# A graph network kernel in which SP, with single-row DMAs, brings one of the 68 gathered tiles of each iteration

## The reference

```
edge_index = jnp.stack([src, dst])
h = jnp.maximum(_layernorm(x, axis=-1), 0.0)
x = x + _L0_gnn_ref(h, edge_index, W_rel, W_root, b_rel)      # agg = segment_sum(h[src], dst); agg @ W_rel.T + b + h @ W_root.T
h = jnp.maximum(_layernorm(x, axis=-1), 0.0)
x = x + _L1_gnn_ref(h, edge_index, edge_attr_50, ...)         # below, with h as its x
edge_weights = jax.nn.silu(edge_features @ We1 + be1) @ We2 + be2
messages = x[src] * edge_weights
agg = jax.ops.segment_sum(messages, dst, num_segments=x.shape[0])
out = jax.nn.silu(agg @ Wn1 + bn1) @ Wn2 + bn2
return x + out
```

## Time and profile before

| | |
|---|---|
| time, median of 3 runs | 5621.94 us (5613.85 to 5627.18) |
| span of the profiled execution | 3996.3 us |
| layer 0, first to last gather issued | 3.5 to 1964.1 us |
| layer 1, first to last gather issued | 2011.3 to 3976.7 us |
| POOL busy | 2976.2 us (74%) |
| PE busy | 2447.1 us (61%) |
| DVE busy | 1995.0 us (50%) |
| ACT busy | 1187.2 us (30%) |

### The profile page before, as it was taken

How to read it: one execution, slowest core, us unless ns; L and a number is a source line. 1 busy time by engine, 2 the same in 40 slices (tenths; PEclk the granted TensorE clock), 3 DMA queues, 4 the chain that set the end, 5 groups by cost and what they waited for, 6 DMA issues and landing times.

```text
span 3996.3 us, 52113 instructions
## 1 busy us (share of the span) xinstructions
PE 2447.1 (61%) x10946; PEld 1882.0 (47%) x10946; DVE 1995.0 (50%) x6931; ACT 1187.2 (30%) x2730; POOL 2976.2 (74%) x3135
## 2 busy tenths in 40 slices
PE   3444444444444444444467788877887777887787
PEld 2334333333433333433445555555555555555555
DVE  6555555555555555555554444444444444444444
ACT  3444444444444444444411111111111111111111
POOL 7777777777777777777567777777777777777776
PEclk8555555555555555555578788788788887888878
DMA  2222222222222222222122222222222222222222
GB/s 84 62 61 61 61 64 67 61 61 61 61 64 67 61 61 61 61 66 64 50 78 78 83 80 79 81 76 83 78 80 82 77 75 83 80 79 82 77 76 82
DMA packets 208083, 284.73 MB, mean 71 GB/s; under 512 B 70338, under 2 KB 137972, under 8 KB 207828
## 3 DMA queue, kind: packets, MB, share of 16 engines
q0 software_dynamic: 100096, 205.20, 18.1%
q1 hardware_dynamic: 66676, 58.00, 4.9%
q10 hardware_dynamic: 41184, 20.45, 1.7%
HBM read 262.97 MB, written 20.45 MB: 71 GB/s over the span
## 4 chain that ended last, share of the span: by engine, by line
POOL 67%; issue 23%; PE 5%; DMA 2%; DVE 1%; POOLq 1%; ACT 0%; SPq 0%; DVEq 0%; ACTq 0%
POOL rows L298 67%; PE hid_ps L368 2%; PE seg_a L330 1%; PE ew_ps L373 1%; DMA rows<-h_rows,idx 1%; PE seg_b L330 1%; DMA ef<-ef_blocks 1%; POOLq L176 1%; POOLq L177 0%; DVE rows L670 0%; DVE onehot L566 0%; DVE ew_ps L666 0%; ACT hidden L502 0%; PE node_t L382 0%; ACT rows L436 0%
## 5 line engine op out<-in xcount | busy, mean ns | idle before, releaser
L298 POOL DMA_INDIRECT rows<-h_rows,idx x1564 | 1490.0, 953 | 522.6 <-issue 515.6
L298 POOL DMA_INDIRECT rows<-x,idx x1564 | 1485.2, 950 | 478.2 <-issue 478.2
L330 PE MATMUL seg_a<-onehot,rows 128*128 128x128 f32 x3312 | 726.6, 388 | 915.0 <-DVE onehot L566 408.1
L330 PEld LDWEIGHTS seg_a<-onehot,rows 128*128 128x128 f32 x3312 | 623.7, 281 | 1148.5 <-issue 960.0
L330 PE MATMUL seg_b<-onehot,rows 128*128 128x128 f32 x2944 | 606.4, 370 | 530.9 <-DVE onehot L566 374.4
L424 ACT ACTIVATE rows<-rows,e_shift,e_rstd 128x128 f32<-128x128 f32 x1564 | 643.3, 481 | 793.0 <-DVE e_shift L593 793.0
L330 PEld LDWEIGHTS seg_b<-onehot,rows 128*128 128x128 f32 x2944 | 520.8, 266 | 727.6 <-issue 448.3
L502 ACT ACTIVATE hidden<-hid_ps,be_col 128x512 f32<-128x512 f32 x391 | 268.8, 687 | 1416.1 <-PE hid_ps L368 1415.8
L373 PE MATMUL ew_ps<-we_sb,hidden 128*128 128x128 f32 x3128 | 539.8, 330 | 49.1 <-ACT hidden L502 49.1
L582 DVE BATCH_NORM_STATS2 e_stats<-rows 128x6 f32<-128x128 f32 x1564 | 339.7, 280 | 426.1 <-DMA rows<-x,idx 361.8
L368 PE MATMUL hid_ps<-ef,we_sb 50*128 50x512 f32 x782 | 522.7, 753 | 39.4 <-DMA ef<-ef_blocks 39.4
(11 more groups left out here) (91 smaller groups left out, 811.5 us busy)
## 6 DMA issues: line engine op xcount, KB each, us to landing
ef<-ef_blocks SPq DMA_DIRECT2D x391, 100.0 KB
rows<-x,idx POOLq DMA_INDIRECT x1564, 2.5
rows<-h_rows,idx POOLq DMA_INDIRECT x1564, 2.5
xs<-x SPq DMA_DIRECT2D x26, 256.0 KB
y_rows<-ys ACTq DMA_DIRECT2D x26, 256.0 KB, 2.5
ys<-y_rows SPq DMA_DIRECT2D x26, 256.0 KB, 3.3
out<-xs ACTq DMA_DIRECT2D x26, 256.0 KB
h_rows<-h1s ACTq DMA_DIRECT2D x24, 256.0 KB, 2.5
```

What stands on the lines that cost most here:

```text
L298: pool.indirect_dma_start(out=rows[:, u, t, :], out_offset=None, in_=table, in_offset=bass.IndirectOffsetOnAxis(ap=idx[:, j:j + 1], axis=0 ...
L330: mm = pe.matmul(seg[u % 2][:, 0:P], rows[:, u, t, :], onehot[:, u % 2, t, :], start=(t == 0), stop=(t == TB - 1))
```

## The change

For the last tile of block 16, tile 67 of an iteration, POOL issues no gather any more: `POOL_TILES` is 67. SP brings its 128 rows, each with a DMA of its own of 512 bytes (`bring_rows`). The row numbers lie in a new tile `sp_idx`, 23 partitions by 128, one partition for each iteration. SP loads them into registers, several with one register load instruction: 16 at a time in layer 0 (8 loads), 10 at a time in layer 1 (12 loads of 10 and one of 8). The DMA's source address is computed from the register.

In layer 0 SP issues all 128 rows behind the load of `xs`, with the first half of `idx` behind the fifth chunk of 16. In layer 1 it issues 10 rows behind each `ef` load from u = 4 on, the last 8 behind u = 16. Ahead of the first row of an iteration SP waits until PE has summed block 16 of the iteration before. The rows count on eight semaphores, 16 rows on each. When all have landed SP raises `s_sp_tile` (`tile_brought`), and DVE waits for it, ahead of the statistics of block 16 in layer 0 and of the product of block 16 in layer 1. Last, it reloads the second half of `idx`. SP also waits for `s_h1_out` ahead of layer 1.

```diff
+CHUNK = 16
+CHUNKS = P // CHUNK
+POOL_TILES = U * TB - 1
...
+            sp.dma_start(sp_idx[:, :], sp_src).then_inc(s_sp_idx, 16)
+            hold(sp, s_sp_idx, 16)
             passes, n_late = load_plan(sp)
+
+            def bring_rows(table, it, first, count):
+                _, sources = nc.values_load_multi_w_load_instructions(
+                    bass.at_runtime_partition(sp_idx[0:1, first:first + count], it),
+                    engines=[mybir.EngineType.SP], min_val=0, max_val=N_NODES - 1,
...
+                for n, v in enumerate(sources):
+                    r = first + n
+                    sp.dma_start(rows[r:r + 1, U - 1, TB - 1, :], table[bass.ds(v, 1), :]
+                                 ).then_inc(s_sp_row[r // CHUNK], 16)
+
+            def tile_brought(layer, tiles):
+                for c in range(CHUNKS):
+                    hold(sp, s_sp_row[c], tiles * (16 * CHUNK) + 16 * CHUNK)
+                sp.sem_inc(s_sp_tile[layer], 1)
...
                     node_x([loop_group(it)], i)
-                    for u in range(HALF):
-                        hold(sp, s_rows[0][u], i * (16 * TB) + 16 * TB)
-                    load_idx(it + 1, 0, HALF, s_idx_a)
+                    hold(sp, s_seg[0], slot_free(i, U - 1, U))
+                    for c in range(CHUNKS):
+                        bring_rows(x, it, c * CHUNK, CHUNK)
+                        if c == CHUNKS // 2:
+                            for u in range(HALF):
+                                hold(sp, s_rows[0][u], landed(i, u))
+                            load_idx(it + 1, 0, HALF, s_idx_a)
+                    tile_brought(0, i)
...
+            ROWS_AT, STEP_ROWS = 4, 10
+            hold(sp, s_h1_out, updates(passes, n_late) * 16)
...
+                        if u == ROWS_AT:
+                            hold(sp, s_seg[1], slot_free(i, U - 1, U))
+                        if u >= ROWS_AT:
+                            first = (u - ROWS_AT) * STEP_ROWS
+                            bring_rows(h1_rows, it, first, min(STEP_ROWS, P - first))
                         if u == HALF + 2:
...
+                    tile_brought(1, passes * ITERS + i)
...
-                    for t in range(TB):
-                        j = u * TB + t
+                    for j in range(u * TB, min(u * TB + TB, POOL_TILES)):
                         pool.indirect_dma_start(
-                            out=rows[:, u, t, :], out_offset=None, in_=table,
+                            out=rows[:, u, j - u * TB, :], out_offset=None, in_=table,
...
-                dve.wait_ge(s_rows[0][u], i * (16 * TB) + 16 * TB)
+                dve.wait_ge(s_rows[0][u], landed(i, u))
+                if u == U - 1:
+                    dve.wait_ge(s_sp_tile[0], i + 1)
...
-                dve.wait_ge(s_rows[1][u], i * (16 * TB) + 16 * TB)
+                dve.wait_ge(s_rows[1][u], landed(i, u))
+                if u == U - 1:
+                    dve.wait_ge(s_sp_tile[1], i + 1)
```

More of the change, by code:

```diff
@@ L79, in build @@
         onehot = sb("onehot", [P, 2, TB, P])
+        sp_idx = sb("sp_idx", [ITERS, P], I32)
         idx = sb("idx", [P, U * TB], I32)
@@ L159, in build @@
         s_mout, s_out = sem("s_mout"), sem("s_out")
+        s_sp_idx, s_sp_tile = sem("s_sp_idx"), [sem("s_sp_tile0"), sem("s_sp_tile1")]
+        s_sp_row = [sem(f"s_sp_row{c}") for c in range(CHUNKS)]
         block = ctx.enter_context(nc.Block())
@@ L172, in slot_free, with landed @@
             return done(i, max(v for v in range(U) if v % slots == u % slots) - U)
+        def landed(i, u):
+            tiles = TB if u < U - 1 else TB - 1
+            return i * (16 * tiles) + 16 * tiles
         def hold(eng, s, value):
@@ L230, in _ @@
                 sp.dma_start(dst[:, :], b.to_broadcast([P, D])).then_inc(s_wts, 16)
+            sp.dma_start(sp_idx[:, :], sp_src).then_inc(s_sp_idx, 16)
+            hold(sp, s_sp_idx, 16)
             passes, n_late = load_plan(sp)
+            def bring_rows(table, it, first, count):
+                _, sources = nc.values_load_multi_w_load_instructions(
+                    bass.at_runtime_partition(sp_idx[0:1, first:first + count], it),
+                    engines=[mybir.EngineType.SP], min_val=0, max_val=N_NODES - 1,
+                    skip_runtime_bounds_check_because="edge sources are node numbers")
+                for n, v in enumerate(sources):
[6 more added lines that the diff above has]
+                sp.sem_inc(s_sp_tile[layer], 1)
             def node_x(groups, n):
```

9 lines of the change are left out of this document (5 added, 4 removed).

## The result

The changed kernel takes 7284.87 us (median of 4 runs, 7276.28 to 7292.54) against 5624.56 for the kernel before (4 runs, 5613.85 to 5627.2). The ratio is 1.2957 [1.2936, 1.2978]. The sign was forecast, the size was not: 6310 had been said, and the range ended at 6560.

A forecast was written before the change was run, and what follows sets the result against it. POOL was taken as the bound, 68 gathers of 1.25 us per iteration, with SP becoming it after the change. Layer 0 +264.6 and layer 1 +423.9 make +688.5, on 5621.9: 6310 us, 8-in-10 range 5570 to 6560.

The forecast's parts named there:

- The base: Whole kernel: changes summed against the span of 3996.3 us, the rest up to the median of 5621.9 taken as unchanged.
- a slower POOL: Rival, outside the span: the unprofiled gather beats at 1.76 us, hiding SP's turns; 5541 us, chance 0.08.
- the rows themselves are dear: Rival, SP's rows: 0.432 us per issue instead of 0.286; 7170 us; chance 0.08, shared with full price per register.
- The row: SP's single-row DMA with address instruction and move: 478 ns each, priced from the `ef` load; 128 take 61.2 us.
- The register load: SP's loads: one trip per register, 2.86 us for 16 and 1.87 for 10 with address instruction and gaps; chance 0.50.
- several registers to a trip: Rival, SP's register loads: with four to a trip, 0.88 and 0.72 us; 5690 us, chance 0.14.
- Layer 0: SP's turn of 96.1 us exceeds POOL's 83.75, so SP is the bound: +264.6 us.
- The forecast's own frame: SP's turn in layer 0: rows, middle, landing, sum of block 16 and waits, 73.25 us, plus eight register loads.
- the point of decision of 1.31: Layer 0: the price in us of one register load at which SP's turn equals POOL's 83.75.
- Layer 1: SP's own work fills the turn: 79.8 us plus 13 register loads of 24.3 together, 104.1 us; +423.9 us.
- The jump back: End of SP's loop in layer 1: a stall of 2.8 us, since SP's body grows longer than DVE's.
- Who waits: Chain on SP instead of POOL; DVE waits for SP's tile ahead of block 16, POOL at its ninth block for `idx`.

The follow-up runs named there:

- experiment 8: On one chip: the kernel before, unchanged, 5673.21 us; the changed kernel 7328.2; the changed kernel with rows from fixed addresses, without register loads, 6096.26.
- experiment 3: Against the changed kernel, each row's DMA writes 16 pieces of 32 bytes to 16 partitions: 4540.06 us, on a chip where the kernel before takes 3993.43.
- experiment 2: Against the changed kernel, the 128 row DMAs read fixed rows, without register loads, address instructions or moves: 3941.62 us.
- experiment 9: Four kernels on one chip, before 5615.69 us: changed 7256.55; changed with register loads at multiples of four 7152.52; without POOL's gathers 4065.01; tile by eight DMAs 5611.41.
- plain_blocks: Against the changed kernel, POOL brings each block with one plain DMA from fixed rows instead of gathers: 4065.01 us, where the kernel before takes 5615.69.
- experiments 2 and 4: Against the changed kernel: the 128 row DMAs from fixed addresses, 3941.62 us; the tile with eight DMAs of 16 fixed rows, 3933.07 us, ratio 0.9848 to before.

## Why the prediction was wrong, point by point

**The base (failed).** "I make the sum against the span and add the difference to the median, as if what lies outside the span stayed as it is." Nothing lies outside. In every run of the experiments the span is 1.8 to 3.0 us below the time of the same run. The page and the times came from chips of two kinds, and the 1.407 between them was the loudest number of the case: something on the timed chip was 1626 us slower. The prediction priced the edit as if the profiled chip were the timed one. The step had a rival, "a slower POOL", and that rival looked at the wrong engine: POOL's gather takes 944 ns on both, and what is slow beside it are SP's queue instructions and the other engines' beginnings. The sum had no term for SP's rows being drawn out beside gathers, and that term is what lifted the result over the range: rows of 125.2 us a turn in layer 0, measured, against 53.8 on an even chip and 61.2 in the forecast.

The sign came out with some luck. On a stretched chip POOL's own turns were 104 and 136 us already (experiment 8), and the forecast's turns for SP, 96.1 and 104.1, lie under both. By that estimate SP at the forecast's prices would have cost nothing there; it cost 1660 us because its rows were drawn out, which the prediction did not have. The rival "the rows themselves are dear" gave 7170, nearest to the 7284.87, and is not what happened: it had each issue at 0.432 us, and the issue's median is 0.225.

**The row (roughly right).** 478 ns forecast, 408 measured on its own: FUSED 37, MOVE 29, DMA 225, gaps 117 together. The `ef` row overstated it: its issue takes 286, that of a row 225, so something between the two forms matters that the prediction held not to. Whether it is the partitions or the bytes no run separates (16 pieces took 316 in experiment 3, one plain row of 2048 bytes 293). With register loads and gaps between groups a tile's rows take 54 us, not 61.2.

**The register load (failed by size).** A trip for each register was given 0.50. Sixteen registers took 1.18 us at the median, not 2.75; ten took 1.15 or 2.29, not 1.76. A window with three loads of layer 0, then one with three of layer 1:

```profile
L228 SPq TENSOR_LOAD <-sp_idx x3: 1166/1167/1167, 204.7 to 220.7; - x3
```

```profile
L228 SPq TENSOR_LOAD <-sp_idx x3: 1117/1142/2271, 2571.6 to 2585.3; - x3
```

8, 12 and 16 registers at 0.72, 0.95 and 1.18 are 0.23 us for each four, and ten, at 1.15, cost more than twelve: two left over seem to cost about 0.2 each, an estimate. So the rival "several registers to a trip" was right in kind for loads that start at a multiple of four, and the forecast for the others, where ten cost 2.29. Both prices stand in the same kernel. Nothing in the trace of before could show alignment; the mistake was to give one form of the price a chance of 0.50 from the split of two numbers, 277 and 305. The Trainium skill (Runtime: NRT & Kernel Launch, Instruction fetch mechanics) gives about 200 ns for each register also in bulk. Here the trace agrees off a multiple of four, 229 ns per register for ten, and not on it, 74 for sixteen.

**Layer 0 (failed on even chips, by the load).** The forecast's own frame, 73.25 plus eight loads, holds: with rows of 53.8 and loads of 10.3 us it gives 76.2, and SP's unhindered turn was 75.1. A load with its address instruction and gaps took 1.29 us, barely under the point of decision of 1.31; what made the room was the cheaper row. Layer 0 is hidden at 83.78. The cheap side had been worked out (80.3, "stays hidden") and given 0.14.

**Layer 1 (right in frame, right in kind).** 79.8 - 61.2 = 18.6 us for all that is neither row nor load; measured on the even chip 96.4 less 54.3 of rows and 23.4 of loads and their address instructions, 18.7. The turn was 96.4 instead of 104.1, and nearly all of the difference is the row.

**The jump back (right).** 2.8 us forecast from DVE's stall. SP's loop of layer 1 on the even chip, around one end (first and last start):

```profile
L275 SPq COMPARE_BRANCH  x1: 53/53/53, 2659.5 to 2659.5; - x1
L275 SPq FUSED_REGOPS  x1: 133/133/133, 2662.0 to 2662.0; - x1
```

2.5 us between the two, 2.4 to 3.1 elsewhere, and 0.2 to 0.3 in experiment 2, whose body is shorter.

**Who waits (right but for POOL's place).** The chain on SP and DVE on `s_sp_tile` are there, on even chips in layer 1 alone. POOL was to stand at its ninth block. It stands longest ahead of its first, 42 and 55 us against 22 and 28 at the ninth in the result's trace, and on the even chip ahead of the first alone, 13 us in layer 1.

**How a reader could have done better.** Correct the row and the load and keep the frame, and the sum is -29 + 245 = +216 us on an even chip; +226 was measured. For the stretched one the trace that was given held no row of a drawn-out instruction. But it held, SP waiting 1875 us beside the gathers, which says that SP's new work would lie inside POOL's runs, and the ratio 1.407. The honest form of that was a wide upper side, since the stretch per instruction was unknown and 384 more instructions a turn were about to be put under it.

## What stays open

That POOL's gathers, issued back to back, go with SP's drawn-out instructions and the other engines' late beginnings on these chips is shown by experiment 9, which takes them away with SP untouched, in one execution. Which part of a gather does it is not: `plain_blocks` differs in the index, in POOL's 0.94 us of writing entries, in their number and in how long POOL issues without a pause. What delays DVE, ACT and PE there, and whether it is the same thing as SP's steps of 0.70 us, is open; the stretched traces also lack some of their semaphore records. Every time of the experiments comes from an execution that gave a span and a clock as well, so no run tells whether the recording has a part in it.

Why some chips show it and others don't is not known either. The same kernel files ran on both kinds, so it isn't the program. Whether it is the chip itself or its condition at that hour can't be told, since each numbered chip was met at one time only.

No version met here beats the kernel before with the tile's rows right. Only those that leave the addressing out do, on even chips (experiments 2 and 4).

## What to carry to other kernels

Compare the profile's span with the timed median before anything else: where they differ by more than a few us, the profile shows another kind of execution than the timed ones, and a price read from it is a lower bound until one execution of the timed kind has been seen. To replace one 1.25 us gather by 384 queue instructions (128 address, 128 move, 128 issue) pays only where the other queue is idle for all of it, here 54 us at its best pace and 125 at its worst. In a bulk register load, start at a multiple of four and take a multiple of four: twelve registers cost less than ten.

## What was not expected of the hardware

- On the result's chip and on three of the five numbered ones, while POOL issued gathers back to back, queue instructions of SP came in steps of about 0.70 us. From start to start an instruction took 0.98 us on average in the changed kernel and 0.84 with fixed addresses (layer 0, chip 1), against 0.14 and 0.30 without. The gathers kept 944 to 947 ns, and their beat of 1.25 where nothing held them. Register operations of DVE kept their length, but one in four of its additions came over 0.5 us late (kernel before, chip 1).
- A register load costs by groups of four and by where it starts: 10 registers 1.15 or 2.29 us, 12 registers 0.95, 16 registers 1.18.
- A single-row DMA issues in 225 ns with a register address, 252 with a fixed one, 316 when cut into 16 pieces, and a row is 0.408, 0.295 and 0.499 us in all.
